# Loading most of x behind the first attention copies, with its statistics at step 2, and the first scores ahead of the second values

## The reference

```
xn = layernorm(x)
q = heads(xn @ Wq.T); k, v = heads(ctx @ Wkv.T)
attn = softmax(where(pad_mask, (q * d**-0.5) @ k.T, -1e9))
x = x + tanh(g_xattn) * (attn @ v)
h = layernorm(x)
top2 = top_k(h @ w_router, 2); score = softmax(top2 logits)
moe = sum over the 2 chosen e of score_e * (silu(h @ fc1[e] proj) * (h @ fc1[e] gate)) @ fc2[e]
shared = (silu(h @ gate_w) * (h @ up_w)) @ down_w
x = x + tanh(g_ffn) * (moe + shared)
```

## Time and profile before

| what | value |
|---|---|
| median of 3 runs | 344.34 us (342.31 to 347.12) |
| the profiled execution's own time | 346.24 us |
| its span, first to last instruction | 344.1 us |
| TensorE busy | 315.4 us, 92% |
| VectorE busy | 241.5 us, 70% |
| ScalarE busy | 170.3 us, 49% |
| mean granted TensorE clock | 0.955 |

### The profile page before, as it was taken

How to read it: one execution, slowest core, us unless ns; L and a number is a source line. 1 busy time by engine, 2 the same in 40 slices (tenths; PEclk the granted TensorE clock), 3 DMA queues, 4 the chain that set the end, 5 groups by cost and what they waited for, 6 DMA issues and landing times.

```text
span 344.1 us, 8044 instructions
## 1 busy us (share of the span) xinstructions
PE 315.4 (92%) x2505; PEld 258.9 (75%) x2505; DVE 241.5 (70%) x725; ACT 170.3 (49%) x322; POOL 119.8 (35%) x133
## 2 busy tenths in 40 slices
PE   8868979999898895878999999999999999999986
PEld 8746758878787784665447488888898898888875
DVE  5556574789796879586779936767667667643795
ACT  2533755586666654546773324544445444423131
POOL 4731111111152625154770053853343433431000
PEclk9967996999999988789999999999999999999999
DMA  8896592946566636410325101333333333202951
GB/s 226 257 216 186 163 245 56 276 152 169 153 179 202 195 128 191 135 68 32 108 94 147 53 15 34 102 98 112 89 105 102 93 97 92 76 27 83 416 177 61
DMA packets 34789, 46.52 MB, mean 135 GB/s; under 512 B 5471, under 2 KB 29411, under 8 KB 34242
## 3 DMA queue, kind: packets, MB, share of 16 engines
q1 hardware_dynamic: 27586, 28.51, 29.8%
q10 hardware_dynamic: 3712, 8.98, 8.3%
q0 software_dynamic: 3456, 8.56, 7.2%
HBM read 21.55 MB, written 12.62 MB: 99 GB/s over the span
## 4 chain that ended last, share of the span: by engine, by line
PE 53%; issue 17%; DVE 7%; POOL 7%; DMA 7%; SPq 6%; ACT 2%; POOLq 0%; DVEq 0%; ACTq 0%
PE ps L1654 25%; PE ps L1322 4%; POOL dispatched L505 4%; SPq L361 3%; DVE x_all L1281 3%; PE ps L1704 2%; PE ps L1626 2%; DMA stacks<-work 2%; PE ps L1523 2%; PE ps L1387 2%; PE ps L1646 2%; PE ps L1532 2%; PE ps L1517 2%; PE ps L1436 2%; PE ps L1370 2%
## 5 line engine op out<-in xcount | busy, mean ns | idle before, releaser
L550 POOL DMA_INDIRECT expert_rows<-v_s,slot_u x39 | 38.3, 982 | 61.9 <-ACT v_s L822 48.1
L917 DVE TENSOR_REDUCE mx<-ps 128x8 f32<-128x1024 f32 x32 | 39.2, 1224 | 23.2 <-PE ps L1387 22.4
L513 POOL TENSOR_TENSOR work<-work 128x512 bf16<-128x512 f32 x16 | 18.5, 1157 | 66.6 <-ACT work L601 66.6
L632 ACT ACTIVATE probs<-ps 128x1024 f32<-128x1024 f32 x32 | 32.6, 1019 | 11.7 <-PE ps L1420 11.7
L1231 DVE TENSOR_TENSOR act<-ps,sil 128x256 f32<-128x256 f32 x39 | 16.6, 425 | 29.5 <-ACT sil L815 29.4
L815 ACT ACTIVATE sil<-ps 128x256 f32<-128x256 f32 x39 | 15.0, 385 | 39.4 <-PE ps L1654 39.3
L1654 PE MATMUL ps<-fc_hi,xs_hi 128*128 x78 | 34.2, 438 | 0.0
L1387 PE MATMUL ps<-stacks 96*128 96x128 bf16 x256 | 22.1, 236 | 10.2 <-DMA stacks<-work 5.3
L1654 PE MATMUL ps<-fc_lo,xs_hi 128*128 x78 | 30.8, 395 | 0.0
L1654 PE MATMUL ps<-fc_hi,xs_lo 128*128 x78 | 30.6, 393 | 0.0
L1387 PEld LDWEIGHTS ps<-stacks 96*128 96x128 bf16 x256 | 17.4, 107 | 15.6 <-DVE mx L917 7.3
(11 more groups left out here) (218 smaller groups left out, 808.0 us busy)
## 6 DMA issues: line engine op xcount, KB each, us to landing
stacks<-work SPq DMA_DIRECT2D x93, 128.0 KB, 3.4
xs_in<-dispatched SPq DMA_DIRECT2D x39, 129.0 KB, 2.1
fc_s<-in_fc ACTq DMA_DIRECT2D x8, 512.0 KB, 3.6
fc_s<-in_fc ACTq DMA_DIRECT2D x8, 256.0 KB, 4.2
stacks<-expert_rows SPq DMA_DIRECT2D x2, 1024.0 KB, 6.4
probs<-expert_rows SPq DMA_DIRECT2D x2, 1024.0 KB, 11.3
ctx_s<-in_ctx_t SPq DMA_DIRECT2D x8, 192.0 KB, 3.3
x_all<-in_x SPq DMA_DIRECT2D x1, 1536.0 KB, 8.7
```

Source lines behind the costliest of these rows:

```text
L513: nc.gpsimd.tensor_tensor(out[:, 2, :], rest, out[:, 1, :], ALU.subtract).then_inc(ready, 1)
L550: nc.gpsimd.indirect_dma_start(ys, bass.IndirectOffsetOnAxis(dst_u[:, r:r + 1], 0), y_out[:, r, :], None, bounds_check=2 * T - 1, oob_is_e ...
L632: nc.scalar.activation(probs[:, 2 * j + h], ps_t, ACT.Exp, scale=HD ** -0.5).then_inc(probs_ok[j][h], 1)
L917: nc.vector.reduce_max(mx[:, j, 8 * h:8 * h + 8], ps_s, AX_X).then_inc(max_ok[j][h], 1)
```

## The change

SP loads only blocks 4 and 5 at the old place, on a semaphore of its own (`x_in2`), and blocks 6 to 15 (1280 KB) behind its last stack copy of group 0. DVE makes the statistics of blocks 4 and 5 in the prologue and those of blocks 6 to 15 at the end of step 2; POOL has a fourth `power1` for them in step 2, ahead of `third(2, ...)`; DVE's `first_norm` for them is the first work of step 3; and `norm1(g)` on ACT waits for the fourth count of `nm_ok` for g = 3 and later. On PE the first scores of group 0 go ahead of the values of group 1.

```
@@ sync
-            sp.dma_start(x_all[:, 4:B, :], x_view[:, 4:B, :]).then_inc(x_rest, 16)
+            sp.dma_start(x_all[:, 4:6, :], x_view[:, 4:6, :]).then_inc(x_in2, 16)
             stack_k(0, 0)
             stack_k(0, 1)
             stack_k(0, 2)
             stack_q(0, 1)
             stack_q(0, 2)
+            sp.dma_start(x_all[:, 6:B, :], x_view[:, 6:B, :]).then_inc(x_rest, 16)
@@ gpsimd
-            power1(4, B, 3)
+            power1(4, 6, 3)
...
                 if live(s - 3):
                     power2(s - 3, 1)
+                if s == 2:
+                    power1(6, B, 4)
                 if live(s):
                     third(s, kst, k_rest, k_ok[1], k_pc, k_ok[2])
@@ scalar
             def norm1(g):
-                sa.wait_ge(nm_ok, min(g + 1, 3))
+                sa.wait_ge(nm_ok, min(g + 1, 4))
@@ vector
-            ve.wait_ge(x_rest, 16)
-            stats(4, B)
+            ve.wait_ge(x_in2, 16)
+            stats(4, 6)
             rest(1, ps_kq, k_ok[0], k_pc, k_ok[2], k_rest, kr_ok)
-            first_norm(4, B, 3)
+            first_norm(4, 6, 3)
...
             for s in range(2, G + 2):
+                if s == 3:
+                    first_norm(6, B, 4)
                 if live(s - 2):
                     maxima(s - 2, 0, 0)
...
                 if live(s - 3):
                     residual(s - 3, 1)
+                if s == 2:
+                    ve.wait_ge(x_rest, 16)
+                    stats(6, B)
                 relink()
@@ tensor
             normed_t(1)
+            scores(0, 0, 0)
             values_proj(1)
-            scores(0, 0, 0)
             scores(0, 0, 1)
```

More of the change, by code:

```diff
@@ L252, in build_program @@
         sums = [ps[:, 4 + t, 0:D] for t in range(CH)]
-        names = """x_in0 x_in1 x_rest ctx_in0 ctx_in1 wq_in wk_in wv_in kones_ok small_in wr_in ffn_in fc1_in fc2_in
+        names = """x_in0 x_in1 x_in2 x_rest ctx_in0 ctx_in1 wq_in wk_in wv_in kones_ok small_in wr_in ffn_in fc1_in fc2_in
             const_ok tanh_ok gates_done zero_row_ok v_ones_ok wr_ok
@@ L275, in two @@
             return [S[f"{name}{j}"] for j in range(2)]
-        x_in0, x_in1, x_rest = S["x_in0"], S["x_in1"], S["x_rest"]
+        x_in0, x_in1, x_in2, x_rest = S["x_in0"], S["x_in1"], S["x_in2"], S["x_rest"]
         wq_in, wk_in, wv_in, kones_ok = S["wq_in"], S["wk_in"], S["wv_in"], S["kones_ok"]
```

## The result

| | before | the change |
|---|---|---|
| median, us | 343.66 (340.93 to 347.12, 6 runs) | 351.17 (348.15 to 352.26, 6 runs) |
| profiled execution's own time, us | 346.24 | 351.73 |
| its span, us | 344.1 | 349.6 |

The change is slower: the ratio to before is 1.022, with a 95% interval of 1.0155 to 1.0284. The interval is clear of 1 but holds 2%, so whether the change is slower by more than 2% stays open; the prediction gave that 0.22. The difference is 7.5 us between the medians, and 5.5 us between the two profiled executions. Forecast were 348.4 us and a range of 345.0 to 352.5. All ratios leave out executions more than 1.5% above the fastest of their kernel on the chip (8 of 17 of before for e1 to e4, 5 of 23 for e5 to e7, 10 of 13 of e6), so medians of all executions are given beside them where the two differ.

The account below looks back on a forecast made before the run. The prediction took TensorE, busy 92% of the span, as the bound, movable through its idle time and clock. -1.1 + 6.1 + 1.3 - 2.3 = +4.0 us gave a median of 348.4 us, range 345.0 to 352.5.

Parts of the forecast that it names:

- rival B: Steps after the stop: clock falls again at about 56, the 2.3 us stay lost; about 351.5 us, chance 0.24.
- Part 1: SP's queue, prologue: without the long load ahead, group 0's last copy lands 1.0 us sooner; the late transfer costs nothing.
- rival C: SP's queue: the long load does not hold SP, so copies land no sooner; 349.4 us, chance 0.15.
- Part 2: TensorE, prologue: first scores ahead of group 1's values; step 2's last scores 1.1 us earlier through an earlier clock rise.
- Part 4: Seam of steps 2 and 3: ten blocks' statistics delay the exponential 6.1 us; low clock behind adds 1.3 us.
- Part 5: TensorE after the stop: the 1.75 us wait and second low clock stretch go, returning 2.3 us (bounds 0 to 2.3).
- A: Prologue: copies land at 20.2, clock stays up, and the early gain outweighs the stop; 343.7 us, chance 0.13.

Follow-up runs that it names:

- e1: The change with TensorE's old order in the prologue, group 1's values ahead of the first scores: 359.47 us, ratio 1.0211 to before.
- e4: The change with the ten BN_STATS at the end of step 2 issued twice: 363.71 us, ratio 1.0282 to before.
- e5: Before with statistics spread over prologue and ends of steps 2 and 3, blocks 8 to 15 loaded behind group 0's copies: 353.58 us, ratio 1.0044.
- e7: Before with statistics spread over prologue, steps 2 and 3, late load of blocks 8 to 15, and first scores ahead of group 1's values: 353.85 us, ratio 1.0113.
- e6: Before with statistics spread over prologue and ends of steps 2 and 3, blocks 8 to 15 loaded ahead of the copies: 354.30 us, ratio 0.9949.
- e8: The change with 90 matmuls of unused result in TensorE's idle time before values(0, 0, 1): 353.50 us, ratio 1.0283 to before.
- e3: Before with statistics of blocks 6 to 15 late as in the change, but load early and TensorE's order old: 357.42 us, ratio 1.0189.
- b2: Before, unchanged, run a third time with a profile: 340.54 us.
- e2: Before with only TensorE's two lines swapped, first scores ahead of group 1's values: 352.55 us, ratio 1.0034.
- b1: Before, unchanged, run once more on another chip than b2: 358.58 us.

## Why the prediction was right, and where its size was off

The direction, the place and the main mechanism (the stop) were right, and the time fell in the range, near its upper end: 351.17 us is where rival B stood (about 351.5), outside the 346.5 to 350 of the forecast itself. The sum was +4.0 us, and the medians show +7.5. Step by step, in the profile:

- **Part 1, SP's queue.** In the change the first six copies took 3.84 us to issue, without the hold, and the last landed 3.69 us after its issue at 17.41: at 21.10, 0.8 us sooner than before (forecast 1.0). But the load alone is not the cause. With it late the same six took 3.84 in the change, e4 and e7, but 5.04 in e1, 4.73 in e5 and 4.88 in e8. With it early they took 4.29 to 5.23 in all eight profiles (4.91, 4.88 and 4.29 in those of before). So the hold was never absent with the early load and present in half of the profiles with the late one; and before had it later too, with no load of x near. That the late load makes it rarer is possible and not shown; rival C's mechanism holds in e1, e5 and e8. The section of the Trainium skill that the prediction set against its own view ("DMA: Bandwidth & Descriptors", anatomy of one DMA) describes transfers that GpSimd issues. These are SP's, so it decides nothing here; what holds SP stays open.
- **Part 1, the transfer costed at nothing.** Wrong by 0.7 us in this profile. The copies of group 1's k landed later behind the 1280 KB, and ScalarE's `first(2, k)` waited 1.79 us for them (34.39 against 33.8 before, with TensorE's keys 0.1 earlier). In e1 it waited 3.38. In e4, e5, e7 and e8, which load late too, it waited for TensorE's keys alone (1.13 us, as before), so this cost is there in two of six profiles. In those two the copies had less spare time than I gave them, for that instruction stands ahead of the statistics, not behind the stop.
- **Part 2, the swap.** Second scores at 25.28 (forecast 25.3), at the low clock. The clock rose at 28.3, 7.1 us after the restart at 21.15, not at 26.1, so the step ends 0.1 us earlier instead of 1.1. The prediction had rows with 5.3 and with 7.3 us from restart to rise and took the first.
- **Part 4, the stop.** Forecast 6.1 us. From the first exponential to the second it was 2.20 us before and 8.44 in the change: 6.24. The same 8.44 stands in e1, and 8.30 in e3. The low clock behind it cost 1.22 us to the scores_t (4.61 against 3.39), forecast 1.3.
- **Part 5, what is given back.** In these two profiles it came: from that scores_t to the next 8.14 us against 9.49, and from there to scores_t(1, 1, 0) 5.92 against 7.73, together 3.16 (forecast 2.3). But 1.35 of it was not forecast: the prediction held the first interval at 9.5 us "at any clock", and it lies between 8.14 and 10.98 in the profiles here. And of the forecast 2.3 only 1.81 came: the second interval is 4.85 us in b2, e2, e6 and e7, and 5.92 in the change, where TensorE waits 1.20 us for stack copies at 60.59 (1.31 in e1, 1.01 in e4, 0.61 in e3, no such wait without the stop). The prediction had no term for that. -0.1 + 0.53 + 6.24 + 1.22 - 3.16 is the 4.7 us of the mark (the 0.53 is the late exponential: 35.04 against 34.61, counted from the keys' 0.1).

**The step that failed is part 5's give-back**, taken as a term of the kernel when it belonged to some executions only. The second low stretch of the profiled one is what the change wins back; of the seven profiles without the ten blocks of statistics at that place, b2, e2, e6 and e7 do not have it (the mean clock is 1.00 from 40 to 60 us), and before, b1 and e5 do. From the second exponential to the mark it is 22.9 to 24.4 us in those three, 19.7 to 20.8 in those four, and 20.9, 21.8 and 20.8 in the change, e1 and e3: behind the stop the change saves some 2 us against the first kind and nothing against the second. The mark itself averages 58.0 us over the seven and 64.7 over the change, e1 and e3, an estimate of +6.7 us for the kernel (executions on several chips, so a rough one). Against an execution without it there is nothing to return: the change's mark of 64.38 stands 9.8 us behind b2's 54.55, some 2.3 of it from b2's quicker prologue (last scores of step 2 at 28.55). The median of before lies 2.6 us under its profiled execution (343.66 against 346.24), and the change's 0.6 under its own (351.17 against 351.73). That difference of 2.0 us is, by arithmetic, the one between the profiled 5.5 and the 7.5 of the medians; that the low stretch makes it is likely and not shown. With the bound 0 for the return, which the prediction kept for its range, the sum would have been +6.3. Which share of the remaining 1.2 us is part 1's and part 2's missing gain (1.7 us in the profile), which is the new wait for copies, less the sooner row, and which is chance, the runs do not separate; that they are of that size is measured in one execution only.

On the clock the Trainium skill ("TensorE: Matmul & The Clock Gate", Part 1) says that one and the same kernel runs a different number of its first matmuls at the low clock from run to run. It says so of a kernel's start, not of its middle. The three profiles of before show the like in the middle (the first low stretch ends at 29.6, 28.1 and 22.3 us, the second is there twice and absent once); had I looked for it there, part 5 would have been a bound.

Of the rivals, A (the early gain outweighs) did not come: the prologue was level. Its sum also left out the 1.3 us of low clock behind the stop that the forecast counts; with them it is +0.7, 345.0 us instead of 343.7. B (the clock not given back) has the right price, +6.3 to +7.4, by another way: in the change's profile the clock was given back, but before had often nothing to give. e8's profile shows B's mechanism itself: a wait of 3.24 us for the row and the low clock behind it.

## What to carry to other kernels

Work moved to "later" must be followed to whoever consumes it first: of ten blocks only two were needed next, and as one batch in front of one semaphore all ten, and a relay over three engines, stood between an exponential and its engine. When one profiled execution lies above its median, look for the term of your sum that it has and the others lack, above all a clock stretch; never count that as a gain. A transfer put in the same queue ahead of copies that feed the next step can hold them up although it ends in time itself; here it did in two of six profiles.

## What was not expected of the hardware

- After a wait of TensorE for the row of maxima the clock fell in the executions with 1.53, 1.75 and 1.77 us of it and not in those with 1.14, 1.25, 1.43 and 1.44 us. The same kernel lies on both sides. That the length of the wait decides is not shown.
- SP's issue of six 128 KB copies took between 3.84 and 5.23 us at the same place in the program. The load of x ahead of it does not explain that alone: with most of it behind them the six took 3.84 us in three profiles and 4.73 to 5.04 in three.
- A row of 12 KB landed 4.71 us after its issue in before, in under 3 us in the change (53.27 to 56.23) and after 6.25 us in e8. The DMA engines were busy throughout in the first and the last (share 1.09 to 1.15), and only until about 54 us in the change (0.70 from 54 to 56); the cause was not tested.
